# Splitting one pair of row tiles into two units of their own, and dealing the later units' slots anew, in a kernel for a decayed neighbour sum

## The reference

```python
support = h @ weight                      # 4096 x 64
mask = (adj != 0)
rank = cumsum(mask, axis=1)
deg = rank[:, -1:]
k = minimum(deg, 100)
pos = rank - (deg - k)
w = mask * where(pos > 0, 0.5 ** (k - pos), 0)
out = x + w @ support + bias
```

## Time and profile before

| what | value |
|---|---|
| median of 3 runs | 216.38 us |
| the profiled execution, its time | 216.8 us |
| its span | 214.2 us |
| PE / PEld busy | 196.7 / 188.0 us (92% / 88%) |
| DVE busy | 196.8 us (92%) |
| ACT busy | 160.6 us (75%) |
| POOL busy | 29.1 us (14%) |
| chain that ended last | PE 81%, DVE 7%, ACT 6% |
| `adj_b` loads | 32, 1 MB each, 35.0 us from issue to landing (median) |
| granted TensorE clock | 0.9 or more of full speed in all 40 slices |

### The profile page before, as it was taken

How to read it: one execution, slowest core, us unless ns; L and a number is a source line. 1 busy time by engine, 2 the same in 40 slices (tenths; PEclk the granted TensorE clock), 3 DMA queues, 4 the chain that set the end, 5 groups by cost and what they waited for, 6 DMA issues and landing times.

```text
span 214.2 us, 6505 instructions
## 1 busy us (share of the span) xinstructions
PE 196.7 (92%) x2784; PEld 188.0 (88%) x2784; DVE 196.8 (92%) x239; ACT 160.6 (75%) x303; POOL 29.1 (14%) x53
## 2 busy tenths in 40 slices
PE   0369979999999999999999999999999999999993
PEld 0269657997898999999999999999999999999993
DVE  1999979797979999999999999989999999998893
ACT  2442996786786988778778778789978989998720
POOL 7800000000010404010004110500000000000000
PEclk9999999999999999999999999999999999999999
DMA  6999999999999999999999999999998000000001
GB/s 203 204 217 220 216 211 216 216 219 212 218 213 221 210 218 216 213 220 216 211 222 212 217 218 215 216 217 218 221 209 174 8 12 3 12 15 3 17 0 43
DMA packets 7677, 36.09 MB, mean 168 GB/s; under 512 B 1506, under 2 KB 3298, under 8 KB 3554
## 3 DMA queue, kind: packets, MB, share of 16 engines
q0 software_dynamic: 4608, 33.56, 75.1%
q1 hardware_dynamic: 2882, 2.10, 3.8%
q10 hardware_dynamic: 160, 0.03, 0.1%
HBM read 68.19 MB, written 1.05 MB: 323 GB/s over the span
## 4 chain that ended last, share of the span: by engine, by line
PE 81%; DVE 7%; ACT 6%; DMA 2%; issue 1%; SPq 0%; DVEq 0%
PE acc L633 40%; PE chain L626 25%; PE chain L624 14%; ACT powers L313 3%; ACT support L296 3%; DMA x_sb<-in_x 2%; DVE masks L358 2%; PE chain L612 2%; DVE sq_sum L460 1%; DVE powers L455 1%; DVE later L399 1%; DVE row_sum L451 1%; DVE part L364 1%; DVE acc L481 0%; DVE sums L364 0%
## 5 line engine op out<-in xcount | busy, mean ns | idle before, releaser
L313 ACT ACTIVATE powers<-chain 128x512 int16<-128x512 f32 (+1 forms) x279 | 148.7, 573 | 33.6 <-PE chain L626 31.4
L633 PE MATMUL acc<-support,powers 128*128 128x192 bf16 x1024 | 159.5, 246 | 1.3 <-ACT powers L313 1.2
L626 PE MATMUL chain<-diag_own,masks 128*128 128x128 bf16 x608 | 107.1, 219 | 0.1
L624 PE MATMUL chain<-diag_past,masks 128*128 128x128 bf16 x568 | 102.2, 219 | 2.1 <-ACT powers L313 1.5
L633 PEld LDWEIGHTS acc<-support,powers 128*128 128x128 bf16 x1024 | 95.9, 98 | 4.3 <-ACT powers L313 2.4
L358 DVE TENSOR_SCALAR masks<-adj_b 128x4096 uint8<-128x4096 bf16 x32 | 72.6, 2281 | 5.0 <-DMA adj_b<-in_adj 5.0
L624 PEld LDWEIGHTS chain<-diag_past,masks 128*128 128x128 fp8e3 x568 | 55.5, 99 | 5.3 <-ACT powers L313 3.9
L626 PE MATMUL chain<-diag_step,masks 128*128 128x128 bf16 x416 | 60.1, 219 | 0.0
L626 PEld LDWEIGHTS chain<-diag_own,masks 128*128 128x128 fp8e3 x608 | 59.7, 99 | 0.3 <-issue 0.3
L626 PEld LDWEIGHTS chain<-diag_step,masks 128*128 128x128 fp8e3 x416 | 39.5, 99 | 0.0
L242 POOL DMA_DIRECT2D adj_b<-in_adj x32 | 24.5, 767 | 108.9 <-DVE masks L358 107.7
(11 more groups left out here) (52 smaller groups left out, 66.3 us busy)
## 6 DMA issues: line engine op xcount, KB each, us to landing
adj_b<-in_adj POOLq DMA_DIRECT2D x32, 1024.0 KB, 35.0
x_sb<-in_x SPq DMA_DIRECT2D x2, 512.0 KB, 4.5
out<-x_sb SPq DMA_DIRECT2D x14, 64.0 KB, 5.4
out<-x_sb SPq DMA_DIRECT2D x4, 32.0 KB, 9.5
w<-in_L_gnn_weight ACTq DMA_DIRECT2D x2, 16.0 KB, 9.1
bias<-in_L_gnn_bias SPq DMA_DIRECT2D x1, 0.2 KB
```

Source lines behind the costliest of these rows:

```text
L313: nc.scalar.activation(powers[:, c, b, cols].bitcast(i16), chain[c][:, cols], ACT.Relu, bias=(MAX_NEIGH + 1) * STEP).then_inc(powers_ready ...
L624: nc.tensor.matmul(chain[c][:, at:at + P], column(n, t + 1), diag_past[:, :], start=False, stop=False, skip_group_check=True)
L626: return nc.tensor.matmul(chain[c][:, at:at + P], column(n, t), diag_own[:, :] if marked else diag_step[:, :], start=False, stop=True, ski ...
L633: return nc.tensor.matmul(acc[u % ACCS][:, k * 3 * D:(k + 1) * 3 * D], powers[:, u % FLIGHT, s + 1 if k < MARKS[u] else s, at:at + P], sup ...
```

## The change

The fourth unit was the pair of tiles 3 and 4. These tiles are now two units of one tile, so that the units are 1, 1, 1, 1, 1, thirteen pairs, 1 (19 units) in place of 1, 1, 1, fourteen pairs, 1 (18 units). Every later pair holds the same tiles as before and each tile is marked or not as before. `STARTS`, `LAGS` and `LEADS` have new values for all units from the third on. Beside the numbers:

- on DVE, `scale(0)` and `scale(1)` stand ahead of `mask(1)`, `scale(2)` and `scale(3)` follow among the halvings, and `scan(1, 0)` stands ahead of `mask(2)`;
- a pair's second mask stands one slot later;
- on ACT, `turn_h(2)` stands ahead of `root()`, `part(3, 0)` moves from slot 2 to slot 4 and `part(1, 2)` from slot 5 to slot 6;
- `halve_2` also waits for the `halve_3` of the unit before;
- the four `acc` buffers become slices of one tensor; tile n's buffer in `adj_b` is `(n + 1) % 8` in place of `n % 8`;
- new code for units that are masked or added in twos is there but is not used, since its two lists (`PAIRED`, `TWINS`) are empty.

```diff
-    SIZES = [1, 1, 1, 2, 2, 2, 2, 2, 2, 2, 2, 2, 2, 2, 2, 2, 2, 1]
+    SIZES = [1, 1, 1, 1, 1, 2, 2, 2, 2, 2, 2, 2, 2, 2, 2, 2, 2, 2, 1]
-    STARTS = [0, 5, 6, 14, 23, 27, 34, 40, 45, 51, 57, 63, 68, 74, 80, 85, 91, 97]
-    LAGS = [8, 5, 9, 10, 9, 10, 9, 8, 9, 8, 10, 12, 11, 11, 11, 10, 9, 8]
+    STARTS = [0, 5, 6, 12, 22, 23, 30, 39, 43, 49, 56, 61, 67, 73, 78, 84, 90, 95, 101]
+    LAGS = [8, 5, 8, 10, 8, 11, 10, 9, 8, 9, 7, 9, 13, 11, 10, 12, 10, 9, 7]
-    LEADS = [0, 0, 0, 0, 0, 0, 0, -1, -1, -1, -1, -1, 0, 0, 0, 0, 1, -1]
+    LEADS = [0, 0, 0, 0, 0, 0, 2, 0, 0, 0, 0, 0, 0, 0, 1, 2, 1, 1, 4]
+    PAIRED = ()
+    TWINS = ()
...
@@ scalar
             turn_h(1)
+            turn_h(2)
             root()
-            turn_h(2)
             turn_h(3)
...
                 if g == 2:
                     part(2, 0)
-                    part(3, 0)
...
                 if g == 4:
+                    part(3, 0)
                     part(2, 1)
                     part(3, 1)
                 if g == 5:
                     part(0, 2)
-                    part(1, 2)
                     part(2, 2)
                 if g == 6:
+                    part(1, 2)
                     part(3, 2)
@@ vector
                 dve.wait_ge(halved, halved_until(u) + 1)
+                dve.wait_ge(sums_ready, u)
...
-                    if u >= 3 and to == 7 and SIZES[u] > 1:
+                    if u >= 3 and to == 6 and SIZES[u] > 1:
```

More of the change, by code:

```diff
@@ L146, in gnn_decay_kernel @@
         chain = [pb(f"chain{c}", [P, 512], fp32) for c in range(FLIGHT)]
-        acc = [pb(f"acc{a}", [P, 512], fp32) for a in range(ACCS)]
+        accs = pb("accs", [P, ACCS, 512], fp32)
+        acc = [accs[:, a, :] for a in range(ACCS)]
         spare = pb("spare", [P, 512], fp32)
@@ L228, in _ @@
             sp.dma_start(bias_1[:, :], bias.rearrange("(a d) -> a d", a=1)).then_inc(bias_loaded, 16)
-            for u in range(NU):
-                sp.wait_ge(rows_done[u % ACCS], u // ACCS + 1)
-                rows = slice(FIRST[u], FIRST[u] + SIZES[u])
+            for u in SETS:
+                sp.wait_ge(rows_done[u % ACCS], sets_until(u))
+                rows = slice(FIRST[u], FIRST[u] + sum(SIZES[v] for v in units_of(u)))
                 sp.dma_start(out_t[:, rows, :], x_sb[:, rows, :]).then_inc(stored, 16)
-            sp.wait_ge(stored, 16 * NU)
+            sp.wait_ge(stored, 16 * len(SETS))
         @block.gpsimd
@@ L241, in load @@
                     pool.wait_ge(mask_ready, n - LOADS + 1)
-                pool.dma_start(adj_b[:, n % LOADS, :], adj_t[n]).then_inc(adj_loaded[n % LOADS], 16)
+                pool.dma_start(adj_b[:, (n + SHIFT) % LOADS, :], adj_t[n]).then_inc(adj_loaded[n % LOADS], 16)
             load(0)
@@ L425, in differ, with rows_of @@
                 nc.vector.tensor_tensor(before, before, after, ALU.subtract).then_inc(weights_ready[c], 1)
[L427 to L431, removed]
+            def rows_of(tensor, u):
+                n, k = len(units_of(u)), SIZES[u]
+                if tensor is x_sb:
+                    return x_sb[:, FIRST[u]:FIRST[u] + n * k, :].rearrange("q (n k) d -> q n k d", n=n)
+                return tensor[:, u % ACCS:u % ACCS + n, 0:k, :]
@@ L502, in _ @@
             halve_3(0)
+            halve_2(0)
             scan(0, 0)
+            scale(0)
+            scale(1)
             mask(1)
-            halve_2(0)
             halve_1(1)
-            scale(0)
+            scale(2)
             halve_2(1)
-            scale(1)
-            scale(2)
             scale(3)
             halve_3(1)
+            scan(1, 0)
             mask(2)
-            scan(1, 0)
             halve_1(2)
@@ L546, in _ @@
                         scan(u, 1)
-                    done = STARTS[u] + LAGS[u] + STEPS[u]
+                    if added_with(u) != u:
+                        continue
+                    done = max(STARTS[v] + LAGS[v] + STEPS[v] for v in units_of(u))
                     if g == done:
```

88 lines of the change are left out of this document (68 added, 20 removed).

## The result

| | before | after |
|---|---|---|
| median of 6 runs each, same chip | 216.36 us (216.13 to 216.53) | 218.38 us (217.71 to 218.55) |
| ratio, with its 95% interval | | 1.0086 (1.0073 to 1.0100) |
| the profiled execution: time, span | 216.8, 214.2 us | 218.36, 216.1 us |
| first product, start of slot 8 | 31.20 us | 31.88 us |
| last product | 210.59 us | 212.47 us |

The change makes the kernel 2.0 us slower, 0.9%. I had forecast 216.2 and a range of 214.9 to 217.7: wrong in sign, and outside the range. The spans of the two traces differ in two pieces: +0.7 us ahead of the first product, +1.2 us of idle PE behind it, 1.9 us in all. (The times of these two executions differ by only 1.6 us, since the one of before took 0.4 more than its median, so the pieces explain the spans and the medians only roughly.)

What follows compares the result with a forecast made beforehand. PE and DVE were taken as full from about 75 us, leaving gains ahead of 73 us. Head +0.35, loops +0.3, scans -0.6, issue gaps -0.2 summed to -0.15 us on the 216.38 median: 216.2 us, range 214.9 to 217.7.

Steps and rivals of the forecast that it cites:

- The loops, slots 8 to 47: PE's idle time in the weigh-and-count loops, new dealing against old: +0.3 us, bounds -1.0 and +1.5.
- reckoning: PE's idle time from slot 8, each slot taking the larger of loop and PE's sum: 5.75 us new, 5.25 before.
- The waits for scans: PE's weight loads waiting for DVE's scans: all scans come in time, so the wait goes, -0.6 us.
- The head: Slots 1 to 8: ACT's waits for scales go but its order gives the gaps back, +0.35 us, first product 31.55.
- the head pays: Faster rival: slot 8's weigh comes as early as ACT's work allows, head -0.9 us; centre 215.2 us, chance 0.30.
- Issue gaps: PE's waits for nothing the profile shows: 0.5 of 0.7 us kept, -0.2 us, bounds -0.7 and +0.5.
- DVE: Slower rival: DVE is the bound behind slot 80, its scans and differs late: 217.6 us, chance 0.18.
- ACT's fixed cost: Rival, slots 12 to 40: two weighs in a row delay the second chain, some 0.05 us a slot: 217.0 us, chance 0.07.

Runs made afterwards that it cites:

- counts-first runs: Kernels before and after, all counts of a chain ahead of its products in each slot: 215.95 us (before) and 216.52 us (after); after, slots 22 to 47 only: 216.89.
- before_cf: Kernel before with each chain's counts ahead of its products in every slot: 215.95 us, ratio 0.9971.
- after_oldparts: Kernel after with part(3, 0) and part(1, 2) back in slots 2 and 5 on ACT, DVE's new head kept: 217.87 us, ratio 1.0050.
- after_warm: Kernel after with 72 idle matmuls on a zeroed tile in PE's first idle stretches: 217.21 us, ratio 1.0020.
- before_cf_warm: Kernel before with counts ahead of products in every slot and 72 idle matmuls in PE's first idle stretches: 216.19 us, ratio 0.9980.
- after_cf: Kernel after with each chain's counts ahead of its products in every slot: 216.52 us, ratio 0.9999.

## Why the prediction was wrong

**The step that failed: "The loops, slots 8 to 47: +0.3 us".** It was +1.15. After, 6.9 us of idle time less the three issue gaps (0.79, 0.35, 0.20) is 5.6, against a reckoning of 5.75. Before, 5.75 less 0.94 of issue gaps and 0.36 of waits for scans is 4.45, against a reckoning of 5.25. So the reckoning held for the new dealing and was 0.8 too high for the old. I had only the old one's trace to hold it against, called it "some 15% high in both" (5.25 over 4.4 is 19%, and for the new dealing there was no trace), and made 0.3 of a difference that my own sums had at 0.5 and that was 1.15.

The 0.8 lies, by the table above and the slots of my working, in slots 30 to 39 and beyond (1.9 reckoned for 30 on, 1.35 there) and in small pieces before them: a likely reason, which no run tests, is that in those slots PE's sum is nearly as long as the loop, and a slot in which PE was behind starts the next loop without waiting. Nothing is wrong in the places: 1.5 us a slot at 25 to 29, 1.7 at 34 to 39. What was missing was the old dealing's idle time taken slot by slot from its own trace, 1.44 us in slots 25 to 29 and 34 to 39 together, to set the new sum of 2.7 for them against (2.8 came, without the issue gap). That these loops are the cause is shown by the counts-first runs: with them short, both dealings have 1.3 us of such idle time.

**"The waits for scans: -0.6 us".** They went, but they were worth 0.36. The 0.6 of the earlier trace rows is PEld's, three times; one of the three is at 28.58, ahead of slot 8, and PE's matmuls were held up by the other two for 0.19 (at 50.15) and 0.17 us (at 57.46).

**The head: +0.35, measured +0.68.** What failed here is that I took the first weigh to come at 19.83 in both kernels; it came at 20.35. Each later step of my working held to 0.2 us when 0.52 us is added: third weigh 24.00 (23.6), fourth 25.45 (25.1), take-offs 26.61 (26.3), PE waiting 0.96 us for `part(3, 0)`. From first weigh to first product it took 11.53 us (11.72 by my working). At equal first weighs the new head costs 0.16 us. The other 0.52 is the clock's late rise in this execution, and it counts against the change all the same, since the old head would have hidden nearly all of it: `before_cf`, with its first weigh at 20.31, began slot 8 at 31.05. I had seen ACT's waits for scales as time to be won and not as room that a late weigh can use. The rival "the head pays" failed on what I had held against it, `part(3, 0)`, and `after_oldparts` shows that DVE's half of it was there to be had, 0.7 us.

**Issue gaps: -0.2, measured +0.4.** I kept 0.5 of 0.7 us, having read one of the three rows of such waits (PEld had 2.3 us of them in all before); start to start on PE there were three gaps of 0.94 us in sum before and three of 1.34 after. I had called them tied to nothing. The trace ties them to something. After, PE around the longest:

```profile
52.08 0.22 PE L693 MATMUL chain<-diag_own,masks 128*128 128x128 bf16 x1
52.92 0.26 PE L700 MATMUL accs<-support,powers 128*128 128x192 bf16 x1 [0.63 <-issue]
```

and the DMA queues between 50 and 51 us (queue, kind: packets, MB, share):

```profile
q8 instruction: 1, 0.02, 6.2%
```

There are 22 such packets of 16 KB in the run. Each gap (from 52.08, 87.83 and 153.59 after; from 94.6, 111.13 and 119.86 before) ends 2.3 to 2.5 us behind the start of one (50.43, 85.93, 151.59; 92.46, 109.23, 117.92), all while the loads keep the DMA engines full. In `after_warm`, where 72 more matmuls shift the code, the packet comes at 52.98 and the gap ahead of slot 25 is gone. So PE's own instructions arriving late is the likely cause; that they do was not tried by itself, and most of the 22 packets leave no gap.

**DVE, ACT's fixed cost.** Neither decided. No PE or PEld row waits for a differ or scan behind 170 us, though DVE is 92% busy. Single-tile slots take 1.11 as before. The Trainium skill ("Perfetto Trace Analysis", Optimizing Scalar/DVE Operations) says that breaking up instructions of an engine that isn't saturated, but causes bubbles on others, may let work be completed sooner. The trace agrees in part: PE's idle time fell where the split pair had stood, from 0.77 to 0.12 us in slots 22 to 24 and from 1.05 to 0.40 in 30 to 33, and rose by 1.4 us in 25 to 29 and 34 to 39 (issue gap left out), where other units' products now stand in a pair's loop.

**The sum.** Head +0.68, loops +1.15, scans -0.36, issue gaps +0.4: 1.9, the difference of the spans. My terms: +0.35, +0.3, -0.6, -0.2. All four are off the same way, and the loops by most.

## What to carry to other kernels

Where one engine's result goes to a second and comes back, compare that loop, with everything that stands between in the first engine's order, with the engine's own sum, slot by slot, and do it for both versions from the trace before a factor is laid on either. Put the work that the second engine waits for ahead of work that nobody waits for: here that order inside a slot was worth 1.9 us in the kernel after, about as much as the change had lost, and 0.4 to 0.6 in the kernel before. A wait that a change removes may have been hiding the lateness of something else: look at how late the work ahead of it can come before the wait is counted as a gain. Once the loops are short, ask what the bases wait for; if that chain begins with a load, what is tuned ahead of it is waited for again there.

## What the runs showed of the hardware

- Float32 matmuls stood 0.21 us apart while the granted clock was 0.50 and 0.11 apart at 1.00 (`before_cf_warm`). In the twelve profiles without idle matmuls ahead the same step in pace came between 16.15 and 18.95 us, where the trace's records of the clock begin; the clock column reads 1.00 ahead of them too, so the pace has to be read.
- With 50 idle matmuls from 1.0 us on, the granted clock rose at 3.77 us in one kernel and stayed up through 3.6 us of idle PE; in another it rose at 4.35, fell at 7.76 in an idle stretch of 3.1 us and rose again at 14.59.
- From the start of the last count of a 128x512 step to the start of the chain's next matmul, with ACT's weigh (0.60 us) between, it takes 0.91 us where that is a count (`after_cf`, 52.55 to 53.46) and 1.00 where it is a product (after, 55.23 to 56.23). So 0.3 to 0.4 us of each loop is not ACT's work.
- PE had gaps of 0.2 to 0.8 us (1.07 in `after_oldparts`), charged to "issue", that end some 2.4 us behind the start of a 16 KB packet on the queue of kind "instruction". With counts first in all slots (`after_cf`) PE has no wait charged to "issue" behind the head.
